# The last seven steps of a software pipeline written out by hand, with twelve expert sums, one low half and two residuals moved from GpSimd to VectorE

## What is computed

```python
x = x + attention(ln(x), mask, Wq, Wk, Wv, Wg, Wo, Wb)
t = x.reshape(tokens)
n = ln(t)
p = softmax(n @ router_w + router_b)
top_p, top_i = top_k(p, 2);  top_p = top_p / sum(top_p)
expert_out = einsum("nd,edc->nec", n, expert_w) + expert_b
t = t + sum_k(top_p[k] * expert_out[top_i[k]])
```

## Time and profile before

| | us |
|---|---|
| three runs, median (lowest to highest) | 859.1 (857.56 to 863.3) |
| the profiled execution | 860.74 |
| its span | 859.0 |
| PE busy in the span | 790.4 (92%) |
| VectorE busy | 756.5 (88%) |
| GpSimd busy | 606.2 (71%) |
| ScalarE busy | 552.0 (64%) |

### The profile page before, as it was taken

The page is one execution under the profiler, slowest core; times in us unless marked ns, Lnnn a source line. Parts: engine busy times, 40 slices in busy tenths (PEclk is TensorE's granted clock), DMA queues, the critical chain, the costliest instruction groups (busy, mean ns, idle before and its releaser), DMA issues.

```text
span 859.0 us, 39278 instructions
## 1 busy us (share of the span) xinstructions
PE 790.4 (92%) x15372; PEld 533.2 (62%) x15372; DVE 756.5 (88%) x1829; ACT 552.0 (64%) x1369; POOL 606.2 (71%) x990
## 2 busy tenths in 40 slices
PE   1999778899999999999999999999999999999743
PEld 1899345666666666666666666666666666666411
DVE  8998535799999999999999999999999999999664
ACT  3887335577667776777667766777677766776331
POOL 7996001378877787778767887778777876778786
PEclk9999989999999999999999999999999999999965
DMA  4563100000211111111111121111111111111000
GB/s 114 193 206 133 55 16 28 26 26 26 64 34 34 34 57 42 34 34 45 53 34 34 33 64 35 33 34 57 41 34 33 42 57 34 34 37 31 25 9 24
DMA packets 32578, 42.46 MB, mean 49 GB/s; under 512 B 6288, under 2 KB 27280, under 8 KB 32400
## 3 DMA queue, kind: packets, MB, share of 16 engines
q1 hardware_dynamic: 31920, 39.95, 14.4%
q10 hardware_dynamic: 480, 0.02, 0.0%
HBM read 13.74 MB, written 6.55 MB: 24 GB/s over the span
## 4 chain that ended last, share of the span: by engine, by line
PE 78%; POOL 9%; issue 6%; DVE 4%; ACT 2%; DMA 0%; POOLq 0%; DVEq 0%; ACTq 0%
PE psS L1120 11%; PE psS L1095 6%; PE ps_x L1151 6%; PE psS L1127 5%; POOL ln_s L376 3%; PE ps_x L1176 3%; PE ps_r L1176 3%; PE psS L1139 3%; PE ps_x L1179 2%; PE ps_r L1179 2%; PE psS L1100 2%; POOL xn L379 2%; PE ps_m L1084 2%; PE ps_o L1251 2%; PE ps_o L1252 2%
## 5 line engine op out<-in xcount | busy, mean ns | idle before, releaser
L827 DVE TENSOR_REDUCE negm<-psS 128x12 f16<-128x1920 f32 x80 | 146.0, 1825 | 14.0 <-PE psS L1105 9.3
L376 POOL TENSOR_TENSOR ln_s<-ln_s,half 128x5 f32<-128x5 f32 (+1 forms) x60 | 86.1, 1435 | 50.6 <-DVE ln_s L883 44.3
L424 POOL TENSOR_TENSOR add<-prod 128x256 f32<-128x256 f32 x160 | 115.0, 730 | 8.8 <-DVE prod L947 8.7
L429 POOL TENSOR_TENSOR add<-add 128x128 f32<-128x128 f32 x200 | 91.2, 456 | 3.3
L583 ACT ACTIVATE gate<-ps_o 128x320 f32<-128x320 f32 x80 | 35.2, 440 | 88.5 <-PE ps_o L1209 88.4
L540 ACT ACTIVATE pt_b<-psS 128x1920 f32<-128x1920 f32 x40 | 70.9, 1771 | 32.1 <-PE psS L1139 32.1
L395 POOL TENSOR_TENSOR xc<-x,ln_s 128x320 f32<-128x320 f32 x40 | 28.9, 722 | 70.5 <-DVE ln_s L876 70.5
L419 POOL TENSOR_TENSOR og_lo<-og,og_hi 128x320 f16<-128x320 f32 x80 | 63.4, 793 | 18.4 <-ACT og_hi L577 18.4
L431 POOL TENSOR_TENSOR ymix<-add 128x64 f32<-128x64 f32 x200 | 63.9, 320 | 15.7
L619 ACT ACTIVATE kept<-ps_r,coef 128x64 f32<-128x64 f32 x320 | 70.0, 339 | 3.2 <-DVE coef L930 2.4
L1095 PE MATMUL psS<-bm,ident 128*128 128x480 f16 (+1 forms) x320 | 68.6, 338 | 3.2 <-issue 2.0
(11 more groups left out here) (279 smaller groups left out, 2847.1 us busy)
## 6 DMA issues: line engine op xcount, KB each, us to landing
xin<-in_x SPq DMA_DIRECT2D x20, 320.0 KB, 3.0
xs_all<-xs_pair SPq DMA_DIRECT2D x20, 320.0 KB, 2.5
xs_q<-xs_all SPq DMA_DIRECT2D x40, 160.0 KB, 2.1
xs_v<-xs_all SPq DMA_DIRECT2D x40, 160.0 KB, 2.4
xin<-in_x SPq DMA_DIRECT2D x40, 160.0 KB, 2.4
out<-res SPq DMA_DIRECT2D x40, 160.0 KB, 2.1
w_raw<-in_expert_w SPq DMA_DIRECT2D x2, 128.0 KB
eb_raw<-in_expert_b SPq DMA_DIRECT2D x15, 2.0 KB
```

Of the source, the lines that this page charges most:

```text
L376: pool.tensor_tensor(ln_s[a][:, 3, 0:w], ln_s[a][:, 2, 0:w], half[:, 0:w], ALU.pow).then_inc(own, 1)
L424: pool.tensor_tensor(add1[t % 2][:], prod_of(t)[:, 0:4, :], prod_of(t)[:, 4:8, :], ALU.add).then_inc(mix_step[t], 1)
L429: pool.tensor_tensor(add2[t % 2][:], add1[t % 2][:, 0:2, :], add1[t % 2][:, 2:4, :], ALU.add).then_inc(mix_step[t], 1)
L827: dve.tensor_reduce(negm[c][:, :, 0:slots], psS[:, :, 0:slots * N].rearrange("i h (s j) -> i h s j", s=slots), AX.X, ALU.max, negate=True) ...
```

## The change

The loop over the steps ends at step 37 on the four compute engines (`END_STEPS`); SyncE keeps its loop. What steps 38 to 44 did is written out as a list of calls for each engine: 80 on TensorE, some 50 on ScalarE and on GpSimd, some 180 on VectorE. All are the same calls as before on the same groups, in another order, except these: VectorE gets functions of its own for some of GpSimd's work, and its list has 12 calls of `mix_all` (groups 35: slabs 1 and 2; 36: 0 and 2; 37: 0 and 3; 38: 0, 1 and 2; 39: 1, 3 and 4), one of `low2` (group 38) and two of `residual` (groups 37 and 39). These are missing from GpSimd's list. Where two engines now count up the same semaphore, each call waits until the count of the group before is reached. `mix_all` is one reduction in place of three additions, and VectorE's new `rinv_low`, `og_low` and `center` are defined but not called.

```diff
-        FIRST, LAST = -2, GROUPS + 5
-        def run_steps(eng, step):
-            for n in range(FIRST, LAST):
+        FIRST, END_STEPS, LAST = -2, GROUPS - 2, GROUPS + 5
+        ENDING = GROUPS - 5
+        def run_steps(eng, step, end=END_STEPS):
+            for n in range(FIRST, end):
                 step(n, n % 2)
...
             def low2(g, a):
                 pool.wait_ge(hi2_ready, g + 1)
+                if g > ENDING: pool.wait_ge(lo2_ready, g)
...
             def mix_halves(g, t):
                 pool.wait_ge(prod_done[t], g + 1)
+                if g > ENDING: pool.wait_ge(mix_step[t], 3 * g)
...
                 pool.wait_ge(mix_step[t], 3 * g + 2)
+                if g > ENDING: pool.wait_ge(base_done, g)
...
+            def low2(g, a):
+                dve.wait_ge(hi2_ready, g + 1)
+                dve.wait_ge(ln2P, 2 * g + 2)
+                dve.wait_ge(lo2_ready, g)
+                dve.tensor_tensor(hl[a][:, 0:T, 1, :], xn[a][:, 0:T], hl[a][:, 0:T, 0, :], ALU.subtract).then_inc(lo2_ready, 1)
+            def mix_all(g, t):
+                dve.wait_ge(prod_done[t], g + 1)
+                dve.wait_ge(mix_step[t], 3 * g)
+                dve.wait_ge(base_done, g)
+                dve.tensor_reduce(ymix[:, t, :], prod_of(t)[:].rearrange("p e d -> p d e"), AX.X, ALU.add).then_inc(mix_step[t], 3)
+            def residual(g, a):
+                for t in range(T):
+                    dve.wait_ge(mix_step[t], 3 * g + 3)
+                dve.wait_ge(base_done, g)
+                need(dve, res_done, g)
+                dve.tensor_tensor(base[:], ymix[:], x1[a][:], ALU.add).then_inc(base_done, 1)
...
+            weigh(GROUPS - 1, 3, ps_o)
+            share(GROUPS - 1, 7)
+            mix_all(GROUPS - 1, 3)
...
```

## The result

The changed kernel takes 847.63 us (median of 4 runs, 845.94 to 850.11) where the kernel before took 858.94 us beside it (857.56 to 863.3): a ratio of 0.9859, with an interval of 0.9832 to 0.9886, so 1.4% faster. The forecast was 848.0.

The account below looks back on a forecast made before the run. GpSimd was taken to bound the last 82.4 us, with VectorE waiting, and VectorE to bound it afterwards. Four stages sum to 71.3 us, so 11.0 us off the 859.0 us span gives 848.0 us, range 843.5 to 855.5.

Parts of the forecast that it names:

- The bound: In the last 82.4 us GpSimd sets the pace, VectorE waiting 20.64 us; after moving 20.5 us, VectorE is the bound.
- rival B: VectorE's waits before logits and attention_out stay, 2 us in each of three stages; 6 us lost, 854 us; chance 0.15.
- S2: Stage from VectorE's logits of group 37 to those of group 38: 16.90 us before, 13.5 forecast.
- The price of a reduction: One mix_all on VectorE, 512 numbers with a step of 64: 0.70 us taken, bounds 0.60 and 1.08.
- Rival A: The reduction on VectorE is dear: 1.08 us gives 852.6; chance 0.15 between 0.9 and 1.62 us, 0.04 beyond.
- Stretched operations: VectorE's small two-input operations, slowed while GpSimd works: four run free, 1.7 us gained in the last two stages.
- The sum: Four stages of the rewritten stretch, forecast at 31.4, 13.5, 13.5 and 12.9 us: 71.3 in place of 82.4.
- S3: Stage from VectorE's logits of group 38 to those of group 39: 15.95 us before, 13.5 forecast.
- four times the slope and the fixed part: Rival A's extreme price of a reduction on VectorE: 2.4 us, giving 868 us, slower.
- C: Rival: the order fills even small gaps, reductions at 0.60 us, no new waits or stretch; 843.5 us; chance 0.04.
- Marks: Signs of being right: mix_all near 0.69 us, given attention_out and logits times, VectorE over 85% busy, base waits under 1.5.
- signs of being wrong: mix_all at 1 us and more, waits over 2 us before logits, or a first stage longer than 32.5 us.

Follow-up runs that it names:

- the contiguous reads: The changed kernel with each moved reduction reading its 512 numbers one after another, summing other numbers, for timing only: 845.88 us beside 860.33 for the kernel before.
- the paired version: The changed kernel with the twelve moved slabs' products written in runs of two numbers, reductions reading at a step of two: 846.98 us beside 859.86 before.

## Why the prediction was right, and where its steps were not

**The bound.** That the drain went at GpSimd's pace was right: every wait for base and for the router in the earlier trace rows is gone, and with GpSimd as full as before the order gains 0.2 us. That "VectorE becomes the bound, and what it pays is the forecast" is half right. Upward it holds (6.23 us of work more, 6.07 us of time); downward a chain of 8.7 to 9.1 us from attention_out to logits stands in the way, which the prediction named under rival B as long as before and did not make a bound, and behind it GpSimd's base again (0.87 us in S2 with cheap reductions).

**The price of a reduction** was the term that was mis-sized: 0.70 us taken, 1.04 measured. The value stood between the contiguous rows and fold's row, and I took the wrong neighbour: fold, the only row that reads with a large step, gave 1.08, and the step decides, not the length. Without a step the same instruction takes 0.68, so the 0.69 was a good price for another instruction. Rival A's words thus came true in price (0.9 to 1.62) and not in time: it would have given about 852. Its rule was the right one, and what it costs here is shown by the contiguous reads, 1.45 us and not 4.4, since the chain and the wait for base hide the rest.

**Stretched operations** were sized at 1.7 us. VectorE's 17 groups on 40 and 80 numbers add up to 25.5 us in the stretch of before and 20.7 in that of the changed kernel, 4.8 less. But with the order alone, and GpSimd as full as ever, they add up to 21.9, and with the moved work alone to 22.8: so the moved work by itself (a lighter GpSimd, as I had argued) brings 2.7, and another order without it 3.6. The mechanism itself shows in rows of the changed kernel (GpSimd and VectorE, by turns):

```profile
830.71 0.86 POOL L444 TENSOR_TENSOR base<-ymix,x 128x320 f32<-128x320 f32 x1 [0.26 <-POOL ymix L437]
...
830.77 0.85 DVE L1026 TENSOR_TENSOR rt<-rt,rs 128x40 f32<-128x40 f32 x1
...
823.45 0.72 POOL L381 TENSOR_TENSOR xn<-xc,ln_s 128x320 f32<-128x320 f32 x1
...
823.69 1.03 DVE L1112 TENSOR_REDUCE ymix<-prod 128x64 f32<-128x512 f32 x1
```

A routing product on 40 numbers, 0.20 us elsewhere, takes 0.85 beside GpSimd's residual of 0.86; a reduction that begins 0.24 us into GpSimd's product of 0.72 takes 1.03, while the last one, beside an idle GpSimd, takes 1.01. So the part of the Trainium skill's section "Who interferes with whom" ("SBUF — State Buffer") that no run had shown, that a reduction never contends, agrees with these rows.

**The sum.** For the stages 31.4, 13.5, 13.5 and 12.9 us were forecast and 31.95, 12.34, 12.82 and 13.80 came: errors of half a microsecond to 1.2 us, of both signs. By the terms of the sum VectorE would work 58.1 + 8.4 (reductions) + 1.5 (low half, residuals) - 1.7 (stretch) = 66.3 us and stand for 5.1. The changed kernel has 66.05 and 4.86. With the reduction at the forecast's price (the paired version: 30.49, 13.01, 12.77 and 13.19, in all 69.46) VectorE works 62.54 and stands 6.92 us. So the rest of the sum held nearly 4 us too much work, most of it the stretch (25.5 to 21.2, thus 4.3 and not 1.7), and nearly 2 us too little waiting: the product that was to wait 0.7 us in S3 waits 0.89, and attention_out 0.87 for base. That is 1.8 us too long in all, and the dear reduction brought 1.45 us back, with 3.51 us more work and 2.06 less waiting. So 71.3 and 70.9 agree in part by luck, because errors have contrary signs. Two side sums of the prediction are slips that bear on nothing here: four times the slope and the fixed part make 2.3 us, not 2.4, and a gain of 3.3 us makes 855.8, not 855.5.

**Rivals.** B did not come: no wait for base or for the router over 0.3 us is left. But it came in each kernel where one half of the change was missing (2.24, 1.20, 2.80 with the order alone, 2.82 with the moved work alone, 1.19 with GpSimd in the old order). C's small gaps exist, but even the paired version doesn't fill them.

**Marks.** Counted from the start of the stretch, which came 3.3 us earlier, attention_out of groups 38 and 39 is at 809.9 and 822.3 (about 809 and 822 forecast), the logits at 806.2, 818.5 and 831.4 (805.6, 819, 832.5); VectorE is over 85% busy in S2 to S4. Only mix_all near 0.69 us is wrong, and one of the signs of being wrong, mix_all at 1 us and more, came.

## What to carry to other kernels

Moving work off a full engine and ordering the rest of the queues are one change: alone the order gave 0.2 us and the moved work 3.7, together 11.5. In the run with the moved work alone, the in-order queue that was set free ran to its next call that wasn't ready. Price an instruction by the row whose access is like it, not by the row whose length is like it, and where a layout may be chosen, let two neighbouring numbers be visited at each place (shown here for writes in runs of two and for a read step of two). When the former bound is gone, look for the next two bounds: work added to the new one costs in full, while work taken from it returns only down to the chain below.

## What was not expected of the hardware

A read of 512 fp32 numbers with a step of 64 costs 1.04 us against 0.68 without, a write with a step of eight 1.08 against 0.68, and both are back at 0.68 where the write goes in runs of two numbers and the read has a step of two. And the length of the drain comes out again within 0.04 us in two executions that differ by 4.4 us in all: what differs between the two is the time before it.
